# A four-layer graph network: node stages of finished chunks run inside the gather passes

## The reference

```
h = relu(layernorm(x)); x = x + gin(h)     # relu(relu((h + sum_edges h[src]) @ W1 + b1) @ W2 + b2)
h = relu(layernorm(x)); x = x + gated(h)   # four steps: a = sum_edges (h @ W[etype].T + b[etype])[src]
                                           #             h = gru(a, h)
h = relu(layernorm(x)); x = x + gcn(h)     # two convolutions: dinv * (sum_edges (dinv * h @ W)[src] + own) + b
h = relu(layernorm(x)); x = x + edge(h)    # per edge: batch norm over all edges of [x_i, x_j - x_i] @ W.T + b,
                                           #           leaky relu, mean per destination
```

## Time and profile before

| | us |
|---|---|
| runs shown, median of 3 | 18168.98 (18140.68 to 18170.34) |
| profiled execution, its own time | 18139.14 |
| its span | 18137.3 |
| busy, share of the span: POOL | 12536.8 (69%) |
| PE | 10054.1 (55%) |
| DVE | 4257.8 (23%) |
| ACT | 570.1 (3%) |

### The profile page before, as it was taken

One profiled execution on the slowest core, in us unless ns is written; L12 is line 12 of the kernel. 1 busy time (PEld: TensorE's weight loads), 2 busy tenths in 40 slices (PEclk: granted clock), 3 DMA queues, 4 the chain that ended last, 5 costly groups with the idle time before them and its releaser, 6 DMA issues.

```text
span 18137.3 us, 185316 instructions
## 1 busy us (share of the span) xinstructions
PE 10054.1 (55%) x40859; PEld 8286.9 (46%) x40860; DVE 4257.8 (23%) x6484; ACT 570.1 (3%) x1419; POOL 12536.8 (69%) x13446
## 2 busy tenths in 40 slices
PE   3454644446444564445644555444544456777799
PEld 3343433334333443344433443333433345666788
DVE  2112211113111131112311123111211113222255
ACT  0000100001000010000100000000000000000000
POOL 7777367774777747777477765777677775777655
PEclk5555555556555565555655555555555555555555
DMA  1111111111111111111111111111111112333322
GB/s 44 26 26 26 29 35 26 26 26 41 26 26 26 26 41 26 26 26 26 41 26 26 26 22 24 26 26 26 27 26 26 26 26 50 80 79 78 77 64 65
DMA packets 742158, 649.05 MB, mean 36 GB/s; under 512 B 467173, under 2 KB 473653, under 8 KB 741766
## 3 DMA queue, kind: packets, MB, share of 16 engines
q0 software_dynamic: 400544, 411.38, 12.0%
q1 hardware_dynamic: 341478, 236.47, 4.6%
HBM read 524.73 MB, written 122.26 MB: 36 GB/s over the span
## 4 chain that ended last, share of the span: by engine, by line
POOL 49%; issue 23%; DMA 14%; PE 12%; DVE 2%; ACT 0%; POOLq 0%; DVEq 0%; ACTq 0%; SPq 0%
POOL RINGF L427 49%; DMA RINGF<-tab_gated,IDX 7%; PE ps L637 6%; DMA RINGF<-tab_gcn,IDX 4%; PE ps L702 2%; DMA RINGF<-tab_edge,IDX 2%; DMA RINGF<-tab_gin,IDX 1%; PE ps L665 1%; PE ps L634 1%; PE ps L734 1%; ACT TEMP L564 0%; DVE TEMP L1008 0%; DVE TEMP L1010 0%; DVE A L1012 0%; DVE TEMP L998 0%
## 5 line engine op out<-in xcount | busy, mean ns | idle before, releaser
L637 PE MATMUL ps<-RINGF,OH 128*128 (+1 forms) x26560 | 6009.6, 423 | 5946.3 <-ACTq L525 5938.6
L637 PEld LDWEIGHTS ps<-RINGF,OH 128*128 128x128 f32 x26560 | 5765.3, 331 | 6824.8 <-issue 6824.8
L427 POOL DMA_INDIRECT RINGF<-tab_gated,IDX x6252 | 5898.9, 944 | 1947.0 <-issue 1749.6
L908 DVE TENSOR_TENSOR A<-A,ps 128x640 f32 x1328 | 1090.7, 821 | 11500.8 <-issue 9837.2
L427 POOL DMA_INDIRECT RINGF<-tab_gcn,IDX x3126 | 2949.3, 943 | 968.2 <-issue 876.4
L634 PE MATMUL ps<-ZERO 1*128 1x512 bf16 (+1 forms) x3819 | 1536.5, 533 | 1152.1 <-issue 1151.4
L915 DVE TENSOR_TENSOR OH<-ps,DLOC 128x1280 f32<-128x1280 f32 x1328 | 1969.5, 1483 | 0.3 <-DVE A L1030 0.2
L427 POOL DMA_INDIRECT RINGF<-tab_gin,IDX x1563 | 1480.9, 947 | 499.6 <-issue 441.9
L427 POOL DMA_INDIRECT RINGF<-tab_edge,IDX x1563 | 1474.8, 944 | 483.2 <-issue 438.0
L634 PEld LDWEIGHTS ps<-ZERO 1*128 1x128 bf16 x3819 | 340.6, 113 | 1683.7 <-issue 1659.8
L774 PE MATMUL ps<-IDX,OH 128*128 (+1 forms) x3320 | 733.4, 353 | 587.0 <-ACT OH L590 587.0
(11 more groups left out here) (152 smaller groups left out, 2777.0 us busy)
## 6 DMA issues: line engine op xcount, KB each, us to landing
RINGF<-tab_gated,IDX POOLq DMA_INDIRECT x6252, 2.4
TEMP<-dloc_dram SPq DMA_DIRECT2D x166, 320.0 KB
kept<-OH SPq DMA_DIRECT2D x166, 320.0 KB, 3.1
RINGF<-kept SPq DMA_DIRECT2D x166, 320.0 KB, 2.9
tab_gated<-TEMP SPq DMA_DIRECT2D x196, 256.0 KB, 2.0
RINGF<-tab_gcn,IDX POOLq DMA_INDIRECT x3126
RINGF<-tab_gin,IDX POOLq DMA_INDIRECT x1563
RINGF<-tab_edge,IDX POOLq DMA_INDIRECT x1563
```

The lines of the kernel that those rows point to most:

```text
L427: nc.gpsimd.indirect_dma_start(out=RINGF[:, at:at + D], out_offset=None, in_=table, in_offset=bass.IndirectOffsetOnAxis(ap=index[:, k:k + ...
L637: return nc.tensor.matmul(ps[:, base:][:, bass.ds(place, width)], onehots_, rows_, start=False, stop=False, skip_group_check=True)
L908: ins = V.tensor_tensor(sums, sums, products_[:, 0:GRP, 0:D], ALU.add)
```

## The change

Nothing runs over the whole array between passes any more, and no pass waits for another's node stages as a block. As the edges are sorted by destination, a block's sum is complete once its last row has been visited. A pass is now written as positions (`positions`): position p has the two groups 2p and 2p + 1 and then one slot of each node stage, with a lag of 0 to 4 positions from stage to stage. There are 83 positions with groups and 49 more without (SLOTS = 83 + 49 = 132). Which chunk a slot works on is read from a table, `CHUNK`, that the kernel computes at the start from the destinations: a chunk is entered in the first free slot at or after the position in which its last visit lies. A slot to which no chunk falls works on one of two spare chunks behind the real ones (blocks 98 to 101, NBX = 102); it does all the work of a slot, its DMA too. SP starts the next gather once the DMAs up to the last real chunk are in (`LASTS`, `table_ready`).

Further parts:
- The ring has 20 batches instead of 16. POOL waits for `ring_free`, which SP counts up from a table (`FREE`) with the exact group after which a batch is through; SP also counts the batches that have landed, in place of ACT.
- `pick` is DVE's and no longer POOL's; ACT issues the chunk DMAs and no longer SP. Each of them loads the chunk's place into a register first.
- The layer norms are done per chunk: DVE `centre` and `scaled`, ACT `root` (two squares with an accumulated sum, one root).
- The two gated tables in DRAM alternate. PSUM: four banks for groups, and one bank each for a stage's tile (no second half).
- A group's place in PSUM is laid out in two banks of five blocks; clearing it is two products of 325 columns instead of three of 512, 512 and 256.
- The edge pass and the last stage are as before but for names and the cleared region.

```diff
+        def positions(eng, span, *stages):
+            def stages_at(p, i, r, tail):
+                for lag, stage in stages:
+                    odd = (r - lag) % 2
+                    if isinstance(p, int):
+                        if 0 <= p - lag < SLOTS:
+                            stage(p - lag, odd, (p - lag) // 2, tail)
+                    else:
+                        stage(p - lag, odd, i + (r - lag - odd) // 2, tail)
+
...
+            for p in range(PEEL):
+                span(p)
+                stages_at(p, p // 2, p % 2, False)
+            with eng.Fori(PEEL // 2, SPAN // 2) as i:
...
+                    span(2 * i + r)
+                    stages_at(2 * i + r, i, r, False)
+            span(SPAN - 1)
+            stages_at(SPAN - 1, SPAN // 2, 0, False)
+            stages_at(SPAN, SPAN // 2, 1, True)
...
+                def free(b):
+                    groups = sp.value_load(FREE[:, bass.ds(b - RING, 1)], min_val=1, max_val=GROUPS)
+                    sp.wait_ge(product, n * GROUPS + groups)
+                    sp.sem_inc(ring_free, 1)
...
+                for h in range(2):
+                    count = sp.value_load(LASTS[:, h:h + 1], min_val=16, max_val=8 * SLOTS)
+                    sp.wait_ge(sent[h], n * (8 * SLOTS) + count)
+                    sp.sem_inc(table_ready, 1)
...
+                    if b >= RING and n < EDGE:
+                        pool.wait_ge(ring_free, n * (BATCHES - RING) + b - RING + 1)
+                        pool.sem_inc(pool_go, 1)
...
-                def body(c, s, i):
-                    if static(i):
-                        pool.wait_ge(chunk_turned, run * NCH + c - 1)
-                        pool.sem_inc(pool_go, 1)
-                    to = PICK[:, s, :, 0:width]
-                    if plus is None:
-                        nc.gpsimd.tensor_copy(to, two(src, c)).then_inc(chunk_picked, 1)
-                    else:
-                        nc.gpsimd.tensor_tensor(to, two(src, c), two(plus, c), ALU.add).then_inc(chunk_picked, 1)
...
-            gather(LAST_PASS, tab_edge, IDX, D, rows_other, 3, e_joined, 0)
+            gather(GIN, tab_gin, IDX, PITCH)
+            for n in (*GATED, MIXED):
+                pool.wait_ge(table_ready, 2 * n)
+                gather(n, tab_gated[n % 2], IDX4, D)
+            pool.wait_ge(table_ready, 2 * CONV)
...
+            def send(n, table, width, done, turn):
+                def stage(s, odd, i, tail):
+                    c = act.value_load(CHUNK[:, bass.ds(s, 1)], min_val=0, max_val=NB + CH)
+                    act.wait_ge(done, turn * SLOTS + s + 1)
+                    nc.scalar.dma_start(chunk_of(by_block(table, width), c),
+                                        TW[:, odd, 0:CH * width].rearrange("p (c f) -> p c f", c=CH)
+                                        ).then_inc(sent[odd], 16)
+                return stage
...
+            for n in GATED:
+                positions(act, no_groups, (1, gates(n)), (3, typed(n)), (0, copied(n, P)), (2, copied2(n, ACT.Copy)),
+                          (3, send(n, tab_gated[(n + 1) % 2], TYPES * D, s_typed, n)))
+            positions(act, no_groups, (1, gates(MIXED)), (0, copied(MIXED, P)), (2, root(1)),
+                      (3, copied2(MIXED, ACT.Copy)), (4, send(MIXED, tab_gcn[0], D, s_conv, 0)))
...
+            def pick(n, clear):
+                def stage(s, odd, i, tail):
+                    c = chunk(s)
+                    if later(s, 2) or n:
+                        dve.wait_ge(s_turned, n * SLOTS + s - 1)
+                        dve.sem_inc(dve_go, 1)
+                    dve.wait_ge(sums, summed(n, s, tail))
+                    dve.sem_inc(dve_go, 1)
+                    width = D if n == GIN else P
+                    V.tensor_copy(PICK[:, odd, :, 0:width], chunk_of(A3, c)[:, :, 0:width]).then_inc(s_picked, 1)
+                    if clear:
+                        dve.wait_ge(s_picked, n * SLOTS + s + 1)
+                        dve.sem_inc(dve_go, 1)
+                        V.tensor_copy(sums_of(c), NONE[:, :, :]).then_inc(sums, 1)
...
+            def centre(turn, s, xs):
+                at = (turn * SLOTS + s) * 3
+                dve.wait_ge(s_ln, at + 1)
+                dve.sem_inc(dve_go, 1)
+                V.tensor_copy(xs, XS[:, :, :])
+                V.tensor_reduce(LN[:, 0, :], XS[:, :, :], AX_X, ALU.add).then_inc(s_ln, 1)
+                dve.wait_ge(s_ln, at + 2)
+                V.scalar_tensor_tensor(CEN, LN[:, 0, :].unsqueeze(2).broadcast_to([P, CH, D]), -1.0 / D, XS[:, :, :],
+                                       ALU.mult, ALU.add).then_inc(s_cen, 1)
+
+            def scaled(n, turn, s, odd, feat):
...
+                V.reciprocal(LN[:, 3, :], LN[:, 2, :]).then_inc(s_ln, 1)
+                dve.wait_ge(s_ln, (turn * SLOTS + s) * 3 + 3)
+                by = LN[:, 3, :].unsqueeze(2).broadcast_to([P, CH, D])
+                if feat is not None:
+                    V.scalar_tensor_tensor(feat, CEN, 0.0, by, ALU.max, ALU.mult)
+                if later(s, 2) or n:
+                    dve.wait_ge(s_turned2, n * SLOTS + s - 1)
+                    dve.sem_inc(dve_go, 1)
+                V.scalar_tensor_tensor(NEXT[:, odd, :, :], CEN, 0.0, by, ALU.max, ALU.mult).then_inc(s_feat, 1)
+
+            def after_mlp(s, odd, i, tail):
+                c = chunk(s)
...
+            def mixed(n, s, odd, feat, at):
+                dve.wait_ge(s_tanh, (n - 1) * SLOTS + s + 1)
+                V.tensor_tensor(ps_gate[:, :, D:2 * D], feat, ps_gate[:, :, 0:D], ALU.subtract).then_inc(s_mix, 1)
+                dve.wait_ge(s_mix, at + 1)
+                V.tensor_tensor(DZ, ps_gate[:, :, D:2 * D], RZ[:, odd, :, D:2 * D], ALU.mult).then_inc(s_mix, 1)
+                dve.wait_ge(s_mix, at + 2)
+
+            def mix(n):
+                def stage(s, odd, i, tail):
+                    feat = feat_of(chunk(s))
+                    mixed(n, s, odd, feat, ((n - 1) * SLOTS + s) * 2)
+                    V.tensor_tensor(feat, DZ, ps_gate[:, :, 0:D], ALU.add)
+                    dve.wait_ge(s_turned2, n * SLOTS + s - 1)
+                    dve.sem_inc(dve_go, 1)
+                    V.tensor_tensor(NEXT[:, odd, :, :], DZ, ps_gate[:, :, 0:D], ALU.add).then_inc(s_feat, 1)
+                return stage
+
...
+            positions(dve, sum_edges(GIN), (0, pick(GIN, True)), (2, after_mlp))
+            for n in GATED:
+                dve.wait_ge(s_feat, n * SLOTS)
+                positions(dve, sum_edges(n), (0, pick(n, True)), (2, mix(n)), (1, pre(n)))
+            dve.wait_ge(s_feat, MIXED * SLOTS)
...
+            positions(dve, sum_edges(MIXED), (0, pick(MIXED, False)), (2, mix_last), (1, pre(MIXED)),
+                      (2, scale_last(MIXED, 1)), (4, convolved(MIXED, 0, 4)))
...
+            positions(dve, sum_edges(CONV), (0, conv_in), (1, convolved(CONV, 1, 1)))
+            positions(dve, sum_edges(LAST), (0, last_in), (2, edge_out))
```

1132 lines of the change are left out of this document (581 added, 551 removed).

## The result

The changed kernel takes 17766.29 us (median of 4 runs, 17764.47 to 17767.7), the kernel before beside it 18169.66 us: ratio 0.9782, 95% interval 0.9765 to 0.9799. The profiled execution has a span of 17762.7 us. The forecast was 17755 us.

A forecast was written before the change was run, and what follows sets the result against it. POOL's gather issues bound the kernel. 18139.1 - 1480 (gaps) + 916 (waits and stalls) + 145 (held issues) + 5 (setup) = 17725 us; with the median 29.8 us above the profiled execution, 17755 us, range 17430 to 18170.

The forecast's parts named there:

- The last term: Whole kernel: the median of the runs shown stands 29.8 us above the profiled execution, taking 17725 to 17755 us.
- What bounds the kernel: All eight passes: POOL issuing 1563 gathers of 1.248 us, 1951 us a pass; nothing else comes near.
- what is removed: Between passes: the seven gaps without a gather, 1480 us; start, end and count of gathers stay.
- the waits for the next table: From a pass's last row to the next gather: 51 (pass 0), 49 (step), 76 (mixed), 20 and 34 us (convolutions).
- Stall = tail of slots less the ring's fill: Pass starts: POOL stalls for slots after the table went out less 247 us: 38, 76 (three times), 250, 0, 72 us.
- the slot of the passes whose ring runs through VectorE: Tail slot as a ring of waits: 6.2 us in pass 0, 10.8 mixed, 4.8 in the second convolution.
- One table load on the ring of the mixed slot: Mixed pass's tail: one table load of 1.28 us counts in the 10.8 us slot, the sigmoid's lies beside it.
- VectorE against POOL's issues: Inside passes: added VectorE operations hold gather issues at two points, 145 us, plus 5 us for the setup's longer lists.
- Hidden tails: Rival, tails: the clock rises, a step's slot is 5.5 us and fits the ring fill, 17490 us; chance 17%.
- Slots a fifth longer: Rival, tails: each tenth on all slots adds about 220 us, nothing gained from 19% on, 18170 us; chance 12%.
- Whole operations: Rival, inside passes: POOL pays whole VectorE operations, 675 us instead of 145, 18285 us; chance 8%.
- PE bound inside the passes: Rival: PE's position over 24 us, each us over costs 580 us over seven passes, 18900 at 2 us; chance 5%.

The follow-up runs named there:

- the table of 84: SLOTS cut to 84, no spare slot behind the last chunk, against the changed kernel with only SLOTS cut from 132 to 86; 16929.37 us, ratio 0.9333.

## Why the prediction was right

The time came out 11 us from the forecast, but large errors cancelled, and that closeness is luck. Against the profiled execution the forecast was 17725 us and 17764.5 was measured: 6 us more for the waits, 138 more for the stalls, 142 less for the held issues, and 37 more since all issues of this execution are 3 ns longer. The last term then gave 28 us back: the median stands 1.8 us above the profiled execution, not 29.8.

- *What bounds the kernel, what is removed, the waits for the next table*: right. 334 us where 328 were forecast, and pass and end keep their length. The slots' share in them is confirmed by the table of 84.
- *Stall = tail of slots less the ring's fill*: right, and shown three times: by fewer slots, by a shorter ring, by shorter slots. It was 138 us too small. The term that was mis-sized is the slot of the passes whose ring runs through VectorE. The price of a register load, taken as 0.8 us, was met; what was missed is a second load in pass 0 (0.53 and 0.60 us in turn in front of L1017, beside 1.21 and 0.85 in front of the pick) and two reads of ACT's accumulator, 0.19 us each, per slot. These are the 0.7 us between 6.2 and 6.9 (in part they lie beside other work). In the mixed pass the idle time in front of the pick is 1.17 and 0.75 us in turn, 0.16 above 0.8 in the mean; with the two reads that explains a part of the 0.8 between 10.8 and 11.6, and the rest stays open, as does the second convolution's 5.6 for 4.8. It is 34 + 34 + 32 us of stall. In a step, whose ring I built from rows of PE and ACT, 7.1 us was met, in part by luck: in every other slot PE's gate products wait for VectorE's mix (L684 for L1046), and with constants for the loads the slot fell to 6.5 us, so VectorE's loads stand on that ring too, where the prediction had none. Its stalls are 9, 9 and 20 us longer than 76, since the first group's product comes behind the tail, and the last step's slots are 7.3.
- *One table load on the ring of the mixed slot*: right (1.3 us a slot).
- *VectorE against POOL's issues*: 150 us forecast, some 10 measured. That there are two points was right (the runs put them at 0.13 and 0.82 us), and so was the difference between copies and operations with two inputs. The failed step is "an issue is held only where one of two points in it falls into the operation, and then for the rest of it and 0.12": the operation must have begun 0.17 us before the first point, 0.31 before the second. For the setup's 1.9 us this changes little, for 0.25 us it takes away nearly all of the price: 0.003 us measured where I took 0.10. The Trainium skill ("SBUF — State Buffer", section "Who interferes with whom") says that a copy in a two-port mode and GpSimd shut each other out for a whole instruction, that issue order decides which waits, and that two SBUF inputs contend only with GpSimd's reads. The runs agree with the hold to the operation's end, with the condition that it began first, in both directions (the copy at 3935.17 waited), and with one point for the tensor_tensor where a copy has two; that the first point is a read and the second a write would follow from it and was not tested. On POOL's side the runs show no lock for the whole instruction: the copy at 2709.57 began 0.49 us into an issue and still held it. What the Trainium skill infers in the same section, that a tensor_tensor leaves descriptor generation alone, does not agree with the row at 4685.42 (1.67 us).
- *Rivals.* Hidden tails: no; the clock did rise in parts of the steps' tails (0.64 in the stall of 86.0 us, between the levels of 1.2 and 2.4 GHz), yet the slot stayed at 7 us, since its ring is mostly hand-overs, ACT and VectorE. Slots a fifth longer: a ninth in pass 0, a fourteenth in the mixed pass, a sixth in the second convolution, none in the steps. Whole operations: refuted. PE bound inside the passes: not on the chip of the result, where a step's position is 21 us as forecast; on two other chips this happened, at 31 us, with the sign that the prediction gave (POOL waits for the ring in mid pass). I had worked its price out and left the chance at 5%, since the profile of one chip can't show how far its sequencers' times hold for the next.

## What to carry to other kernels

When work moves from between the passes into them, its tail is free only as long as the producer has room to run ahead: compare (slots left) x (slot) with the ring's fill, and make the number of slots as small as the data allow before anything else (here 4.5% of the time on the first chip, twice what the change itself gave). Build the length of a slot from the ring of waits, with every register load as an operation of 0.8 us on it. A pipeline in which an engine keeps up by a few us per position rests on its sequencer's times: measure it on more than one chip, and read a tail's slots separately for the stretch in which the producer runs and for the stretch after it.

## What the hardware showed that was not expected

- An indirect issue of 0.944 us can be held by VectorE at two points, 0.13 and 0.82 us into it (the second by copies and tensor_scalars, not by operations with two SBUF inputs), until the operation ends, if it began 0.17 us (first point) or 0.31 us (second) ahead; copies of 0.244 us cost it 0.003 us each, copies of 0.687 us 0.19. In return a copy that starts between 0.52 and 0.77 us into an issue is made longer, by up to 0.26 us.
- A register load in front of an operation leaves VectorE idle for 0.5 to 1.2 us.
- On two chips 14 to 15% of SP's register, branch and semaphore instructions and 7 to 10% of VectorE's and PE's lasted 0.6 to 0.8 us, where most take 0.02 to 0.07, and nearly all of these stand beside POOL's gathers: a slot of the same tail took some 30 us there and 7 us once POOL stood still. The kernel before took 21574 and 21623 us on these chips, 18140 to 18170 otherwise.
